# Weight stages of a four-layer graph network: block masks loaded for four pairs of groups at a time, and one-head source rows issued alternately from SP and ACT

## The reference, cut to what matters

```python
# L1_gnn, L2_gnn: twice gat_layer (4 heads, then 1 head)
def gat_layer(x, src, dst, W, a_src, a_dst, bias, heads, out_ch):
    xW = (x @ W).reshape(n, heads, out_ch)
    alpha_s = jnp.sum(xW * a_src, axis=-1)
    alpha_d = jnp.sum(xW * a_dst, axis=-1)
    e = jax.nn.leaky_relu(alpha_s[src] + alpha_d[dst], SLOPE)
    m = jax.ops.segment_max(e, dst, num_segments=n)
    w = jnp.exp(e - m[dst])
    z = jax.ops.segment_sum(w, dst, num_segments=n)
    alpha = w / z[dst]
    out = jax.ops.segment_sum(xW[src] * alpha[:, :, None], dst, num_segments=n)
...
# L3_gnn: once, with 4 heads and one maximum over all edges
e = jax.nn.leaky_relu(s_src[src] + s_tgt[tgt], 0.2)
exp_e = jnp.exp(e - jnp.max(e))
```

## Time and profile before

| | us |
|---|---|
| three runs | 9665.90, 9672.11, 9689.99 |
| median | 9672.11 |
| profiled execution | 9659.98 |
| its span, first to last instruction | 9658.3 |
| PE busy in it | 6492.2 (67%) |
| DVE busy in it | 5133.1 (53%) |
| ACT busy in it | 2741.6 (28%) |
| POOL busy in it | 3646.3 (38%) |

### The profile page before, as it was taken

The page is one execution under the profiler, slowest core; times in us unless marked ns, Lnnn a source line. Parts: engine busy times, 40 slices in busy tenths (PEclk is TensorE's granted clock), DMA queues, the critical chain, the costliest instruction groups (busy, mean ns, idle before and its releaser), DMA issues. The chain is left out here.

```text
span 9658.3 us, 89308 instructions
## 1 busy us (share of the span) xinstructions
PE 6492.2 (67%) x25974; PEld 4040.2 (42%) x25974; DVE 5133.1 (53%) x10543; ACT 2741.6 (28%) x6163; POOL 3646.3 (38%) x3646
## 2 busy tenths in 40 slices
PE   6848587799577556479965645655843777547766
PEld 6824233344455434347743333433441333223344
DVE  7832475323788654621067555455664888543221
ACT  0112100222355133112224432331233555233311
POOL 2635577001277367230054745750120555110111
PEclk5569656899799766679987776656976999768878
DMA  4200233010377333125433324320030222200022
GB/s 110 71 6 11 60 104 100 31 40 20 107 204 204 91 111 103 38 74 171 146 96 97 103 73 136 102 68 3 25 115 20 78 68 68 80 20 4 8 77 73
DMA packets 440397, 752.07 MB, mean 78 GB/s; under 512 B 172541, under 2 KB 268763, under 8 KB 437489
## 3 DMA queue, kind: packets, MB, share of 16 engines
q0 software_dynamic: 182080, 437.26, 16.5%
q1 hardware_dynamic: 239699, 288.90, 9.3%
q10 hardware_dynamic: 18136, 20.19, 0.6%
HBM read 666.38 MB, written 79.35 MB: 77 GB/s over the span
## 5 line engine op out<-in xcount | busy, mean ns | idle before, releaser
L2619 POOL DMA_INDIRECT R<-table,edges x1248 | 1228.2, 984 | 602.9 <-issue 299.8
L2671 DVE TENSOR_TENSOR acc<-acc,PS 125x256 f32 (+3 forms) x1664 | 705.5, 424 | 772.5 <-PE PS L2688 656.7
L2688 PE MATMUL PS<-R,hot 128*125 128x256 f32 (+1 forms) x1664 | 799.5, 611 | 244.8 <-ACT R L2631 72.7
L2688 PEld LDWEIGHTS PS<-R,hot 128*125 128x125 f32 x1664 | 400.9, 281 | 642.5 <-DMA R<-table,edges 253.9
L2631 ACT ACTIVATE R<-R,TW 128x128 f32<-128x128 f32 (+1 forms) x1248 | 493.6, 431 | 552.1 <-DMA R<-table,edges 549.7
L2437 PE MATMUL PS<-S,hotT 125*128 125x100 bf16 (+1 forms) x6240 | 352.8, 214 | 417.5 <-DVE hotT L2544 403.9
L2619 POOL DMA_INDIRECT xx<-table,edges x416 | 417.8, 1004 | 362.8 <-PE PS L2688 292.0
L1918 POOL DMA_INDIRECT sorted_edges<-edge_rows,edge_place x391 | 401.7, 1027 | 323.3 <-DVE edge_place L2156 114.0
L2686 PE MATMUL PS<-R,hot 128*125 128x258 f32 x1664 | 411.3, 398 | 140.3 <-DVE acc L2669 128.4
L2437 PEld LDWEIGHTS PS<-S,hotT 125*128 125x128 bf16 x6240 | 302.3, 110 | 468.6 <-DVE hotT L2544 377.7
L2619 POOL DMA_INDIRECT room<-table,edges x416 | 407.4, 979 | 239.3 <-PE PS L2688 147.2
(11 more groups left out here) (739 smaller groups left out, 13581.5 us busy)
## 6 DMA issues: line engine op xcount, KB each, us to landing
rowb<-slo_row SPq DMA_DIRECT2D x260, 250.0 KB
W<-in_L_ffn_W1p SPq DMA_DIRECT2D x32, 1024.0 KB
W<-in_L_ffn_W2p SPq DMA_DIRECT2D x32, 1024.0 KB
near<-dst_row SPq DMA_DIRECT2D x98, 256.0 KB
R<-table,edges POOLq DMA_INDIRECT x1248, 2.8
W<-in_L_ffn_w SPq DMA_DIRECT2D x16, 1024.0 KB
hib<-hi_mask SPq DMA_DIRECT2D x260, 50.0 KB, 9.8
g<-gate_rows POOLq DMA_DIRECT2D x8, 1568.0 KB
```

Source lines behind the costliest of these rows:

```text
L2619: pool.indirect_dma_start(self.R[:, u, 0:self.W], None, self.table[:, :], bass.IndirectOffsetOnAxis(ap=self.G.edges[:, g, 0:1], axis=0)).t ...
L2671: v.tensor_tensor(to, to, self.G.PS[0:P, self.bank + k, 0:self.WH], ALU.add).then_inc(self.put, 1)
L2688: mm = pe.matmul(self.G.PS[0:P, self.bank + k, 0:self.WH], hot, self.R[:, u, :], start=True, stop=True)
```

## The change

With MP = 4 a mask load brings the masks of four pairs (1600 B a partition, 13 loads a stage instead of 52) into one of RM buffers: three with one head, two with four. The issue of piece q comes after row k = 4(q - 1), or the first row after that; it waits for `taken` to reach 8(q - RM + 1). With one head the even rows stay on SP and the odd ones are issued by ACT at the start of its stream, with the same waits; with four heads all stay on SP. `take` reads its piece by number. Three small tiles are allocated only where they are used.

```diff
--- before.py
+++ after.py
@@ -2344,13 +2344,13 @@
 
 
 
-    TH, RR, RM, NQ = T * H, 6, 8, ET // 4
+    TH, RR, RM, MP, NQ = T * H, 6, 3 if H == 1 else 2, 4, ET // 4
     fill = G.fills[H]
     lag = 14
     with Stage(nc) as s:
         S3, rest = s.sb("S3", [P, 3, H, T], BF16), s.sb("rest", [P, H, T])
         rowb = [s.sb(f"rowb{j}", [P, 1024], BF16) for j in range(RR)]
-        hib = [s.sb(f"hib{j}", [128, 8, T], BF16) for j in range(RM)]
+        hib = [s.sb(f"hib{j}", [128, 8 * MP, T], BF16) for j in range(RM)]
         hotT = [s.sb(f"hotT{j}", [P, 512], BF16) for j in range(3)]
         prod = [s.sb(f"prod{j}", [128, 4, H, T]) for j in range(2)]
         S1 = s.sb("S1", [128, ET, H])
@@ -2360,7 +2360,8 @@
         L = s.sb("L", [TT, CT, H, 128]) if spare is None else spare[0:TT, 0:CT, :].unsqueeze(2)
         rowF, rowI = [[rowb[2 * x + j][0:H, :].bitcast(F32)[:, 0:ET] for j in range(2)] for x in range(2)]
         sc = s.sb("sc", [TT, 2, CT, H])
-        one, top, wide = s.sb("one", [TT, 1]), s.sb("top", [1, 1]), s.sb("wide", [TT, 1])
+        if everywhere:
+            one, top, wide = s.sb("one", [TT, 1]), s.sb("top", [1, 1]), s.sb("wide", [TT, 1])
         got, got_hi = [s.sem(f"got{j}") for j in range(RR)], [s.sem(f"got_hi{j}") for j in range(RM)]
         far, apart = s.sb("far", [P, 512], BF16) if H > 1 else None, s.sem("apart")
         hot_odd = s.sem("hot_odd")
@@ -2373,6 +2374,14 @@
         for g in range(CT):
             chunk_at[min(ready_at[g] + lag, NQ)].append(g)
         flat = lambda a: a[:, :, :, :].rearrange("p c h q -> p (c h q)")
+
+        def rows(eng, k):
+            if k >= RR:
+                eng.wait_ge(hot, (k - RR + 1) * (1 if H > 1 else 2))
+                if H > 1:
+                    eng.wait_ge(hot_odd, k - RR + 1)
+            eng.dma_start(rowb[k % RR][:, :], over(G.slo_row[k * 1024:(k + 1) * 1024], P)).then_inc(got[k % RR], 16)
+
         with nc.Block() as block:
             @block.gpsimd
             def _(pool):
@@ -2394,26 +2403,23 @@
 
             @block.sync
             def _(sp):
-                def rows(k):
-                    if k >= RR:
-                        sp.wait_ge(hot, (k - RR + 1) * (1 if H > 1 else 2))
-                        if H > 1:
-                            sp.wait_ge(hot_odd, k - RR + 1)
-                    sp.dma_start(rowb[k % RR][:, :], over(G.slo_row[k * 1024:(k + 1) * 1024], P)).then_inc(got[k % RR], 16)
-
-                def masks(k):
-                    if k >= RM:
-                        sp.wait_ge(taken, 2 * (k - RM + 1))
-                    sp.dma_start(hib[k % RM][:, :, :].rearrange("p j b -> p (j b)"),
-                                 G.hi_mask[:, k * 8 * T:(k + 1) * 8 * T]).then_inc(got_hi[k % RM], 16)
-                for k in range(RR - 1):
-                    rows(k)
-                    masks(k)
-                masks(RR - 1)
-                for k in range(RR - 1, NQ // 2):
-                    rows(k)
-                    if k + 1 < NQ // 2:
-                        masks(k + 1)
+                def masks(q):
+                    if q >= RM:
+                        sp.wait_ge(taken, 2 * MP * (q - RM + 1))
+                    sp.dma_start(hib[q % RM][:, :, :].rearrange("p j b -> p (j b)"),
+                                 G.hi_mask[:, q * MP * 8 * T:(q + 1) * MP * 8 * T]).then_inc(got_hi[q % RM], 16)
+                rows(sp, 0)
+                masks(0)
+                for k in range(1 if H > 1 else 2, RR - 1, 1 if H > 1 else 2):
+                    rows(sp, k)
+                for q in range(1, RM):
+                    masks(q)
+                q = RM
+                for k in range(RR - 1 if H > 1 else RR, NQ // 2, 1 if H > 1 else 2):
+                    rows(sp, k)
+                    if q < NQ // 2 // MP and k >= MP * (q - 1):
+                        masks(q)
+                        q += 1
 
             @block.tensor
             def _(pe):
@@ -2473,6 +2479,8 @@
 
             @block.scalar
             def _(act):
+                for k in range(1, NQ // 2, 2) if H == 1 else []:
+                    rows(act, k)
                 for n in range(1, NQ, 2) if H > 1 else []:
                     act.wait_ge(got[(n // 2) % RR], 16 * (n // 2 // RR + 1))
                     if n >= 3:
@@ -2503,11 +2511,12 @@
 
                 def take(n):
                     v.wait_ge(gathered, n + 1)
-                    v.wait_ge(got_hi[(n // 2) % RM], 16 * (n // 2 // RM + 1))
+                    q, j = divmod(n, 2 * MP)
+                    v.wait_ge(got_hi[q % RM], 16 * (q // RM + 1))
                     if n >= 2:
                         v.wait_ge(summed, n - 1)
                     v.tensor_tensor(prod[n % 2][:, :, :, :], PS[:, n % 4, 0:4 * TH].rearrange("p (f h b) -> p f h b", f=4, h=H),
-                                    hib[(n // 2) % RM][:, 4 * (n % 2):4 * (n % 2) + 4, :].unsqueeze(2).to_broadcast([128, 4, H, T]),
+                                    hib[q % RM][:, 4 * j:4 * j + 4, :].unsqueeze(2).to_broadcast([128, 4, H, T]),
                                     ALU.mult).then_inc(taken, 1)
 
                 def total(n):
```

## The result

| | us |
|---|---|
| before, median of 4 runs | 9671.25 |
| after, median of 4 runs (9808.62 to 9831.70) | 9809.85 |
| ratio | 1.0142, 95% interval 1.0127 to 1.0156 |
| profiled execution of after, its span | 9831.70, 9830.0 |

The change makes the kernel slower by 138.6 us. The forecast was 9780 with a range of 9725 to 9840. The profiled execution is itself 22 us above the median of its kernel. Between the two profiles about 25 us of the difference stand in the sums over edges after the first weight stage (547 us before, 572 after), which the change doesn't touch.

The account below looks back on a forecast made before the run. DVE was taken to bound the four-head stages, and 125-partition row DMAs on five of 16 engines the one-head stages. 122 - 3.5 - 4 = +115 us gave 9775 from the profiled execution, 9787 from the median; forecast 9780, range 9725 to 9840.

Parts of the forecast that it names:

- The bound of the one-head stages: One-head stages: DVE waits 66.4 and 59.4 us for rows, as a 125-partition load gets five of 16 DMA engines.
- Part 1: One-head rows alternately on SP and ACT: bandwidth gain 0, rows landing in twos cost about +1.2 us per stage.
- part 2: Masks loaded four pairs at a time: gain 0 to 5 us per one-head stage, nothing with four heads.
- Part 3: Four-head stages: rows stand behind a piece's wait for its buffer, stalling DVE 40.7 us per stage, +122 us for three.
- the small stall at piece 2: Four-head stages: piece 2 is due with one pair more in hand, so DVE stands only 2.0 us.
- the chunk: Four-head stages: piece 6's wait is hidden behind DVE's first chunk of scans, costing 0.
- the other nine: Four-head stages: the nine remaining piece waits stall DVE 4.3 us each, 38.7 us per stage.
- The chunk's wait for dT: First four-head stage: the first chunk, arriving later, no longer stands 3.54 us for dT's DMA: -3.5 us.
- A: One-head stages: two queues carry twice as much, -118 us; total 9672, or 9630 with a small stall; chance 0.04 each.
- B: Four-head stages: the new wait is covered, leaving -4 us and a total of 9668; chance 0.05.
- C: Four-head stages: gathers and fills beside the burst make each stall 5.5 us, total 9823; chance 0.87 together with the forecast.
- its own reading of the shares: DMA engines: 125-partition rows alone reach a share of 0.33, two queues of 125-partition tiles together 0.32, 128-partition loads 1.04.

Follow-up runs that it names:

- c3: The kernel before, with POOL's early gathers left to the next stage, rows over 125 partitions: 9753.72 us, ratio 1.0067 to the kernel before.
- c2: The kernel before, with no early gathers and row loads over 128 partitions instead of 125: 9686.24 us, ratio 1.0007 to the kernel before.
- e2: The changed kernel, with four-head mask pieces issued five rows later: 10142.71 us, ratio 0.9995 to the kernel before.
- e3: The changed kernel, with four-head mask pieces issued one row later: 10198.32 us, ratio 1.0053 to the kernel before.
- c4: The changed kernel, with four pieces of two pairs instead of two of four in the four-head stages: 9675.46 us, ratio 0.9993 to the kernel before.
- b4: The kernel before, with only the odd rows of one-head stages issued by ACT: 10071.41 us, ratio 0.9986 to the kernel before.
- e1: The changed kernel, with four-head stages loading masks as before, so only one-head stages are changed: 10151.15 us, ratio 0.9999 to the kernel before.
- b1: The kernel before, with row loads over 128 partitions instead of 125: 10092.03 us, ratio 1.0018 to the kernel before.
- b3: The changed kernel, with rows over 128 partitions and four-head pieces issued five rows later: 10081.69 us, ratio 0.9992 to the kernel before.
- e4: The changed kernel, with row loads over 128 partitions instead of 125: 10209.64 us, ratio 1.0058 to the kernel before.
- r1: The changed kernel again without edits, on a slower chip: 10200.12 us, ratio 1.0116 to the kernel before.

## Why the prediction was right, step by step

- **The bound of the one-head stages** (five engines for a 125-partition load, whichever queue): right. The change itself left the waits for rows where they were, with the two queues' shares together at the old one; c3 against c2 shows that 128 partitions free the rows on the same queue. The rule of the Trainium skill in "DMA: Bandwidth & Descriptors", section "Why a DMA increments its semaphore by 16 and not by 1", by which 125 partitions use five engines and 128 use 16, agrees with both. The Trainium skill's remark on the same page, section "Issuing engines are not separate DMA queues", that a second issuer saves only issue time, agrees with the shares of 32.6% and 35.3%.
- **Part 1 and part 2**: -4 us forecast, -1.5 + 1.1 = -0.4 measured in the two stages. Rows do land in twos, 5.1 us apart where gathers run beside them (4.2 forecast). Nothing of the up to 5 us a stage that longer mask packets could have given is visible.
- **Part 3, the place**: right. Eleven waits a stage, the small stall at piece 2 (2.4, 1.7 and 2.6 us against 2.0), next to none at the chunk (0, 0 and 0.9 us), and the other nine at full size. e2 removes them by place alone, e3 halves them, c4 removes them by number of pieces.
- **Part 3, the size**: forecast for the three stages were 122 - 3.5 = +118.5 us, and they grew by 144.9, 26 us more. The mis-sized term is the way of a row from the end of the wait to DVE. Taken as 4.93 + 0.4 = 5.3 us, it measured 6.0 on average (5.6 to 6.4, once 7.75), and the 27 full stalls 4.9 us instead of 4.3: 16 of the 26 us. The issue of the piece, 0.44 us, was about as taken; the row's own way from its issue to DVE was 5.2 to 5.9 us (once 7.3) instead of 4.93. That the 200 KB piece just ahead of it takes time on the same engines is likely; no run separates it. Two smaller terms had been put at nothing: the first rows of each stage, whose waits rose from 3.7 to 3.8 us to 4.7 to 4.9 (3 us in all), and waits for later rows of a burst (12.5 us against 7.9 before). The chunk's wait for dT went in all three stages, 3.54 + 0.66 + 2.18 = 6.4 us instead of 3.5. Some 5 us of the 26 aren't placed.
- **The sum**: +115 forecast, +138.6 measured. By the stages of the two profiles the growth is 144.5, 30 us more than forecast: the 26 above, and the gain of part 2 of which only 0.4 us came. The medians show 6 us less than the profiles' stages, which isn't explained. The upper bound of 5.5 us a stall held for the average and for 26 of the 27.
- **Rivals**: A fell with the waits for rows in the one-head stages of after and with c3 and c2 (its condition, rows standing for the queue); b4 and e1 agree but weigh less. B fell with the waits view of after. C was the truth in part: its 9823 lies nearer to the measured 9810 than the forecast's 9780 does, but most of the extra came in every stall alike, with or without gathers beside it, and only one reached C's 5.5 us.
- What the forecast saw and didn't use: a 128-partition load of the rows was within reach of its own reading of the shares.

## What to carry to other kernels

A load that has long to wait for its buffer must not stand ahead of loads that are needed sooner: in one issuer's stream, place it where its wait is already over, or else count how much of the other stream is in hand when it stops, and compare that with the whole way of a load, not with its transfer time. Before spreading loads over queues, look at the share of the DMA engines that one load reaches alone: here it was a third of them; the partition count was the cure (128 for 125), and a second queue was worth nothing. And a stage that gets shorter shows its next holder at the barrier, here the gathers issued ahead.

## What the runs showed of the hardware that was not expected

- The kernel before took 9671 and 9674 us on two occasions and 10154 and 10089 on two others. In the slower sets DVE and PE lose time while POOL issues its scatters and gathers: a pair of groups at the start of a stage takes 3.7 to 4.5 us instead of 2.3, and where POOL issues without a pause DVE can stand up to 26 us (b1; 31 us in b3) after PE has finished what it waits for, with no packet of a row or mask moving in those looked at. What it waits for there stays open.
- A row of 2 KB copied to 128 partitions lands sooner than one copied to 125, though it is 6 KB more: in the stalls of the first four-head stage it reached DVE 3.6 to 4.1 us after its issue in e4, and 5.3 to 6.2 in r1. After the first chunk of the one-head stage DVE gets through a pair in its own 1.2 us in c2, and in c3 mostly in the 2.1 to 2.2 us at which rows land. How much quicker the rows could come in c2 isn't seen, as DVE bounds there.
